# Layer-1 attention rebuilt: four heads in row and column groups of the array

## The reference, cut to what matters

```python
q = x @ Wq.T + bq; k = x @ Wk.T + bk; v = x @ Wv.T + bv
qm = q.reshape(d_batch * NB_HEADS, q_len, d_head)      # 16 heads of width 8, 256 tokens
att = jnp.einsum('nqd,nkd->nqk', qm, km)
att = jax.nn.softmax(att, axis=-1)
att_out = jnp.einsum('nqk,nkd->nqd', att + batch_pos, vm)   # a bias added after the softmax
att_out = att_out.reshape(d_batch, q_len, d) @ Wo.T + bo
att_block = layer_normalize(att_out + x)
ff = (att_block @ W1.T + b1) @ W2.T + b2
return layer_normalize(ff + att_block)
```

## Time and profile before

| what | us |
|---|---|
| median of 3 runs | 1746.96 |
| lowest, highest | 1745.7, 1750.88 |
| the profiled execution, its own time | 1739.43 |
| its span, first to last instruction | 1737.6 |
| first and last start of a score matmul (L1716) in it | 1224.0, 1610.3 |

### The profile page before, as it was taken

How to read it: one execution, slowest core, us unless ns; L and a number is a source line. 1 busy time by engine, 2 the same in 40 slices (tenths; PEclk the granted TensorE clock), 3 DMA queues, 4 the chain that set the end, 5 groups by cost and what they waited for, 6 DMA issues and landing times. The chain is left out here.

```text
span 1737.6 us, 31729 instructions
## 1 busy us (share of the span) xinstructions
PE 1351.8 (78%) x8970; PEld 1077.2 (62%) x8970; DVE 1112.3 (64%) x2581; ACT 939.1 (54%) x2747; POOL 812.6 (47%) x824
## 2 busy tenths in 40 slices
PE   2267786697877984897998998994899988999552
PEld 0044564464645764897998897992566666676452
DVE  4575787877978544648447547442578888888522
ACT  1155564565756763666666666662556555555110
POOL 2446646555475312564665564663344544432103
PEclk7588898888988986999999999996889899989576
DMA  6300000000000005020020000006111111220063
GB/s 211 106 2 3 1 9 3 7 9 0 8 2 7 9 7 205 20 109 10 10 103 15 11 12 8 13 9 193 35 22 31 26 24 34 33 31 10 12 194 112
DMA packets 127182, 72.28 MB, mean 42 GB/s; under 512 B 78296, under 2 KB 118488, under 8 KB 126680
## 3 DMA queue, kind: packets, MB, share of 16 engines
q1 hardware_dynamic: 116664, 60.95, 12.3%
q0 software_dynamic: 3200, 6.56, 1.5%
q10 hardware_dynamic: 7200, 3.41, 0.7%
HBM read 53.26 MB, written 17.12 MB: 41 GB/s over the span
## 5 line engine op out<-in xcount | busy, mean ns | idle before, releaser
L1433 POOL TENSOR_TENSOR hl<-hid,hh 128x256 fp32r<-128x256 f32 x396 | 293.2, 742 | 221.2 <-ACT hh L1410 217.4
L1476 DVE SCALAR_TENSOR_TENSOR hid<-GU,gub,sg 128x256 f32<-128x256 f32 x396 | 190.3, 481 | 194.5 <-ACT sg L1404 111.8
L1304 PE MATMUL GU<-xh,wh 128*128 128x256 f32 x792 | 233.5, 295 | 39.4 <-DVE wl L1452 30.3
L1404 ACT ACTIVATE sg<-GU,gub 128x256 f32<-128x256 f32 x396 | 188.2, 475 | 123.6 <-PE GU L1306 122.1
L1305 PE MATMUL GU<-xl,wh 128*128 128x256 f32 x792 | 225.6, 285 | 0.0
L1306 PE MATMUL GU<-xh,wl 128*128 128x256 f32 x792 | 225.6, 285 | 0.0
L1840 ACT ACTIVATE prob<-S,negmax 128x256 f32<-128x256 f32 x256 | 119.2, 470 | 164.3 <-DVE negmax L2225 162.2
L1304 PEld LDWEIGHTS GU<-xh,wh 128*128 128x128 f32 x792 | 152.4, 192 | 48.9 <-issue 27.1
L1410 ACT CAST hh<-hid 128x256 fp32r<-128x256 f32 x396 | 158.1, 399 | 27.0 <-DVE hid L1476 25.8
L1716 PE MATMUL S<-kpad,qn 128*128 128x512 f32 x256 | 152.0, 679 | 1.5 <-POOL kpad L1960 1.4
L1305 PEld LDWEIGHTS GU<-xl,wh 128*128 128x128 f32 x792 | 152.8, 193 | 0.0
(11 more groups left out here) (289 smaller groups left out, 3263.9 us busy)
## 6 DMA issues: line engine op xcount, KB each, us to landing
raw<-in_expert_w SPq DMA_DIRECT2D x4, 2688.0 KB, 12.3
modb<-mod_d SPq DMA_DIRECT2D x2, 2688.0 KB, 15.0
list<-zero SPq DMA_DIRECT2D x5, 1024.0 KB, 9.7
raw<-in_expert_w SPq DMA_DIRECT2D x4, 1152.0 KB, 6.6
wa<-in_w SPq DMA_DIRECT2D x16, 256.0 KB, 3.5
wb<-in_w SPq DMA_DIRECT2D x16, 256.0 KB, 4.3
kpad<-rel_d SPq DMA_DIRECT2D x1, 3072.0 KB, 13.3
qkv_d<-qkvT SPq DMA_DIRECT2D x24, 128.0 KB, 4.5
```

The costliest lines, as they stand in the source:

```text
L1304: pe.matmul(out, lhs[0], rhs[0], start=start, stop=False, skip_group_check=True)
L1404: act.activation(sg[:, c % BUFS], GU[c % BUFS][:, 0:TT], ACT.Silu, bias=gub[:, GATE, e * CH0 + c:e * CH0 + c + 1]).then_inc(silu, 1)
L1433: pool.tensor_tensor(hl[:, b], hid[:, b], hh[:, b].bitcast(F32), ALU.subtract).then_inc(hid_lo, 1)
L1476: dve.scalar_tensor_tensor(out=hid[:, c % BUFS], in0=GU[c % BUFS][:, TT:2 * TT], scalar=gub[:, UP, e * CH0 + c:e * CH0 + c + 1], in1=sg[:, ...
```

## The change

`RowBank`, the slots and their loop are gone. `Turns` orders the uses of a bank by a number, and every engine walks through 109 steps written out in full, 8 to a row; `row_at(step, offset)` says which row has a given piece of work in a step. A step carries half a quad: two of the 16 heads, for all 256 queries.

- Keys and queries lie as `KA` and `QA`, each head in its own group of 32 partitions: 8 rows of features and a ninth. Four heads (a quad) stand one above the other.
- `scores` issues eight matmuls in a step: four for the scores by query into `S` (two heads), which only serve the maximum, and four for the scores by key into `ST` (two heads of four steps earlier), which feed the exponential. The four heads lie in four different groups of rows.
- `maxima` takes one reduction over 1024 elements a partition. `tops` (on PE and DVE) transposes the negated maxima and adds them into the ninth row of `QA`, where the ninth row of `KA` is one, so that scores by key come out with the maximum already subtracted.
- ACT takes one exponential over 1024 elements a step. The transposes of the probabilities, their copy, the sums, the reciprocals and the pass of `add_bias` over the probabilities are gone.
- `av` uses V as weights, nine columns for each head (the ninth is one and yields the sum), and runs four heads in four groups of columns: eight matmuls with the bias `B` moving, eight with the probabilities moving. ACT copies the result to `OE`.
- SP sends `qkv` out in 6 DMAs and reads `KA`, `QA` and `vT` back in 9; it sends `OE` out in 8 and reads `ol` back in 2. Division by the sum and the sum of both parts happen afterwards on 128 x 256 (steps 1 to 3 of `step_a`).
- Q, K and V come from two matmuls with hT as weights and 384 columns moving, and DVE adds their bias (`add_bias`, now another function). The padded keys are gone from POOL; the mixing of layer 0's expert outputs moves from DVE to POOL (`mix_outputs`), and POOL now waits for `w_in` before it gathers.

```diff
+        bankE = Turns(sem("te_full"), sem("te_drained"), {"hT": -9.5, "qkv0": -8.5, "qkv1": -7.5, "vT": 3.5, "pos": 29.5})
+        bankL = Turns(sem("tl_full"), sem("tl_drained"), {"oT": 17.5, "wo": 18.5, "router": 27.5, "aT": 20.5, "uT": 21.5, "w2": 22.5})
+        bankN = Turns(sem("nm_full"), sem("nm_drained"), {"top0": 2, "top1": 4, "top2": 6, "top3": 8, "h2T": 26.5})
...
+            def step_program(step):
+                b = row_at(step, -7)
+                if b is not None:
+                    bankE.wait_emptied(sp, "qkv1", b)
+                    of = io["qkv_d"][b].rearrange("(k d) (l c) -> l k d c", d=ROWS, c=16)
+                    for t in range(TILES):
+                        for k in range(3):
...
                     take_waits(sp, taken)
-                    sp.dma_start(io["att_d"][bass.ds(l, 1)].rearrange("o (p x) -> (o p) x", p=P), attT[:]).then_inc(att_out, 16)
-                    sp.wait_ge(att_out, 16 * (l + 1))
+                    if b >= 2:
+                        sp.wait_ge(t_mm, STEPS * (b - 1))
                     take_waits(sp, taken)
-                    if not known_zero(l):
-                        bankL.wait_full(sp, "wo", slot - 1)
+                    for k, to in ((K_, KA), (Q_, QA)):
+                        for j in range(4):
+                            sp.dma_start(to[32 * j:32 * j + ROWS, b % 2],
+                                         io["qkv_d"][b, k * ROWS:(k + 1) * ROWS].rearrange("d (g j x) -> d g j x", j=4, x=NT)[:, :, j]).then_inc(qk_in, 16)
+                    bankE.wait_full(sp, "vT", b - 1)
                     take_waits(sp, taken)
...
-                if E:
-
-                    bankE.wait_emptied(sp, "v", slot)
+                    sp.dma_start(vT[:], io["qkv_d"][b, V_ * ROWS:V_ * ROWS + DH1].rearrange("d (h x) -> (d h) x", x=NT)).then_inc(v_in, 16)
+                b = row_at(step, 13)
...
+                    of = io["o_d"][b].rearrange("(o d) (g j x) -> d g j o x", d=ROWS, j=4, x=NT)
+                    for j in range(4):
+                        for o in range(2):
+                            sp.dma_start(of[:, :, j, o], OE[32 * j:32 * j + ROWS, b % 2, :, o * NT:(o + 1) * NT]).then_inc(o_sent, 16)
+                    sp.wait_ge(o_sent, 128 * (b + 1))
                     take_waits(sp, taken)
-                    if not known_zero(b):
-                        sp.wait_ge(reord, 2 * b)
-                        take_waits(sp, taken)
-                        sp.wait_ge(k_pad, 4 * b)
+                    if b >= 1:
+                        sp.wait_ge(dA, NA * (b - 1) + 3)
                     take_waits(sp, taken)
-                    sp.dma_start(qkvs[:], io["qkv_d"][bass.ds(b * 3, 3)].rearrange("k (p x) -> p k x", p=P)).then_inc(qkv_in, 16)
-                    sp.wait_ge(qkv_in, 16 * (b + 1))
-                    take_waits(sp, taken)
-
-            over_rows(sp, slot_program)
...
+            def scores(step):
+
+                s, t = halves_at(step)
+                if s:
+                    row, i = s
+                    if i == 0:
+                        pe.wait_ge(qk_in, 128 * (row + 1))
+                        if row == 0:
+                            pe.wait_ge(B_out, B_STEPS)
+                    if STEPS * row + i > 0:
+                        pe.wait_ge(s_max, STEPS * row + i)
+                if t:
+                    row, i = t
+                    if i % 2 == 0:
+                        bankN.wait_emptied(pe, f"top{i // 2}", row)
+                    if STEPS * row + i > 0:
+                        pe.wait_ge(t_exp, STEPS * row + i)
+                for blk in range(2):
+                    for e in range(2):
+                        if s:
+                            row, i = s
+                            j, g = 2 * (i % 2) + e, i // 2
+                            mm = pe.matmul(S[:, e, blk * NT:(blk + 1) * NT], QA[32 * j:32 * j + DH1, row % 2, g, blk * P:(blk + 1) * P],
+                                           KA[32 * j:32 * j + DH1, row % 2, g, :], start=True, stop=True)
+                            if blk == 1 and e == 1:
+                                mm.then_inc(s_mm, 1)
+                    for e in range(2):
+                        if t:
+                            row, i = t
+                            j, g = 2 * (1 - i % 2) + e, i // 2
+                            mm = pe.matmul(ST[:, e, blk * NT:(blk + 1) * NT], KA[32 * j:32 * j + ROWS, row % 2, g, blk * P:(blk + 1) * P],
+                                           QA[32 * j:32 * j + ROWS, row % 2, g, :], start=True, stop=True)
+                            if blk == 1 and e == 1:
+                                mm.then_inc(t_mm, 1)
+
+            def tops(row, quad):
+                pe.wait_ge(s_max, STEPS * row + 2 * quad + 2)
+                bankN.wait_drained(pe, f"top{quad}", row)
+                for q in range(2):
+                    mm = pe.transpose(NM[:, q * P:(q + 1) * P], top_now[:, quad % 2, q, :], ident)
+                mm.then_inc(bankN.full, 1)
+
+            def av(row, quad):
+                if quad == 0:
+                    bankE.wait_emptied(pe, "vT", row)
+                if QUADS * row + quad > 0:
+                    pe.wait_ge(o_out, QUADS * row + quad)
+                for kb in range(2):
+                    for j in range(4):
+                        head = 4 * quad + j
+                        pe.matmul(O[32 * j:32 * j + ROWS, NT:2 * NT], V[:, row % 2, kb, head, :],
+                                  B[:, head, P * (1 - kb):P * (1 - kb) + NT], start=(kb == 0), stop=(kb == 1), skip_group_check=True)
+                pe.wait_ge(t_exp, STEPS * row + 2 * quad + 2)
+                for kb in range(2):
+                    for j in range(4):
+                        mm = pe.matmul(O[32 * j:32 * j + ROWS, 0:NT], V[:, row % 2, kb, 4 * quad + j, :],
+                                       pT[:, quad % 2, j, kb, :], start=(kb == 0), stop=(kb == 1), skip_group_check=True)
                 mm.then_inc(o_mm, 1)
 
```

```diff
+                    row, i = t
+                    act.wait_ge(t_mm, STEPS * row + i + 1)
+                    done = QUADS * row + i // 2 - 1
+                    if i % 2 == 0 and done > 0:
+                        act.wait_ge(o_mm, done)
+                    first = 2 * (1 - i % 2)
+                    act.activation(pT[:, (i // 2) % 2, first:first + 2].rearrange("p j k q -> p (j k q)"),
+                                   ST[:].rearrange("p e x -> p (e x)"), ACT.Exp).then_inc(t_exp, 1)
+                now = quad_at(step, 6)
+                if now:
+                    row, quad = now
+                    act.wait_ge(o_mm, QUADS * row + quad + 1)
+                    if row >= 2 and quad == 0:
+                        act.wait_ge(o_sent, 128 * (row - 1))
+                    act.copy(OE[:, row % 2, quad, :], O[:]).then_inc(o_out, 1)
+                b = row_at(step, 28)
+                if b is not None:
+                    act.wait_ge(dB, NBS * b + 11)
+                    act.activation(ex[:], lm[:], ACT.Exp).then_inc(g_exp, 1)
+
...
+            def mix_outputs(b):
+                weights = keep["mixw"][:, b * TILES:(b + 1) * TILES, :, None].broadcast_to([P, TILES, 2, D])
+                pool.wait_ge(gathered, 64 * (b + 1))
+                pool.tensor_tensor(ya[:], ya[:], weights, ALU.mult).then_inc(mix, 1)
...
+            def maxima(row, i):
+
+                dve.wait_ge(s_mm, STEPS * row + i + 1)
+                quad = i // 2
+                if i % 2 == 0 and QUADS * row + quad >= 2:
+                    before = QUADS * row + quad - 2
+                    bankN.wait_full(dve, f"top{before % QUADS}", before // QUADS)
+                first = 2 * (i % 2)
+                to = top_now[:, quad % 2].rearrange("p q (j c) -> p j q c", j=4)[:, first:first + 2, :, DH1]
+                dve.tensor_reduce(to, S[:].rearrange("p e (q k) -> p e q k", q=2), X, ALU.max, negate=True).then_inc(s_max, 1)
+
+            def tops(row, quad):
+                bankN.wait_full(dve, f"top{quad}", row)
+                of = QA[:, row % 2, quad, :]
+                dve.tensor_tensor(of, of, NM[:, 0:NT], ALU.add).then_inc(bankN.drained, 1)
+
...
+            def add_bias(b, t):
+                bankE.wait_full(dve, f"qkv{t}", b)
+                if t == 0 and b >= 1:
+                    dve.wait_ge(qkv_out, 96 * b)
+                dve.tensor_tensor(qkv[:, t, :], TE[:, 0:3 * D], b3[:], ALU.add).then_inc(bankE.drained, 1)
+
...
+            at_e = {-14: (1, 2, 3), -11: (4, 5, 6), -9: (7,)}
+            at_a = {17: (1, 2, 3), 19: (4, 5, 6), 20: (7, 8), 23: (9, 10, 11), 24: (12, 13, 14)}
+            at_b = {25: (1, 2, 3), 26: (4, 5, 6), 28: (7, 8, 9, 10, 11), 29: (12, 13, 14, 15), 30: range(16, 29)}
...
+            def step_program(step):
+                s, _ = halves_at(step)
+                if s:
+                    maxima(*s)
+                now = quad_at(step, 2)
+                if now:
+                    tops(*now)
```

(61 more changed lines are left out.)

661 lines of the change are left out of this document (269 added, 392 removed).

## The result

The changed kernel takes 1723.83 us (median of 11 runs, 1716.86 to 1730.35), the kernel before 1745.7 (11 runs on the same chip, 1733.58 to 1750.88): ratio 0.987, 95% interval 0.984 to 0.989. It is faster by 22 us, 1.3 per cent, where 106 were forecast, and lies above the range. Its profiled execution took 1716.86 us, with a span of 1715.1; it is the fastest of the 11.

A forecast was written before the change was run, and what follows sets the result against it. DVE, with PE close behind, bounds the kernel; a full row falls from 51.5 to 38 us (30.3 DVE, 3.6 waits, +2 clock, +2 disturbances). Heads -116, start +6, end +4: 1633, forecast 1640; range 1595 to 1700.

The forecast's parts named there:

- a quarter: Share of time PE sits at the lower clock level in a full row, against a seventh before; +2 us a row.
- PE at the lower clock: Rival, chance 0.08: nearly the whole stretch at the lower level, scores 2.3, `av` 3.9, row 51 us plus waits; 1755.
- row groups run four at a time: Scores on PE: a step's 16 records in four groups of 32 rows take 1.2 us; bounds 1.1 and 4.5.
- DVE's reduction: Maxima on DVE: each reduction of 1024 elements takes 1.22 us, eight make 9.8 us a row.
- ACT's exponential: ACT in a row: 8 exponentials of 1.08 us, 14 us with copies and small ones; never last.
- SP's chain: SP's DMA issues and landings within a row: 22 us, with seven of eight steps, 33 us, to hide in.
- PE's small products: PE in a row: some 9 us of small products, from 44.6 less scores, `av` and transposes.
- four same-step waits: PE waits for DVE's result in steps 1 (`att`), 2, 5 and 0: 1.5, 0.5, 0.9, 0.7, together 3.6 us a row.
- The end: From the last `av` to Wo: 11 us instead of 7.1, with 8 issues, 2 issues and two landings; +4.
- The start: Before the first scores: POOL gathers behind `w_in`, mixing follows, 15 issues instead of 4; +6 us.
- two at a time: Rival, chance 0.12: only two row groups run together, scores take 2.3 us; row 44, 1685.
- Waits cost more: Rival, chance 0.16: same-step waits or SP's chain cost 10 us a row instead of 3.6; row 45, 1690.

The follow-up runs named there:

- k32: Changed kernel with the scores' matmuls over all 32 rows of each group, the added rows holding zeros; 1673.82 us, ratio to before 0.957.
- k16: Changed kernel with the scores over 16 rows of each group instead of 8 and 9, the added rows holding zeros; 1688.23 us, ratio to before 0.966.
- nobias: Changed kernel with the eight `av` matmuls on the bias `B` left out, so the result lacks the position bias; 1712.57 us, ratio to before 0.979.
- bias2: Changed kernel with the eight bias matmuls of `av` issued twice; 1711.55 us, ratio to before 0.979.
- lateonly: Changed kernel with only the three small PE groups (oT, h2T, positions) issued one step later, behind the next scores; 1685.33 us, ratio to before 0.965.
- late: Changed kernel with scores over 32 rows, POOL gathering before `w_in`, and three small PE groups behind the next step's scores; 1645.17 us, ratio to before 0.943.
- early: Changed kernel with POOL waiting for `w_in` only before its first mixing, no longer before its first gather; 1716.18 us, ratio to before 0.982.
- late2: As late, with the second Q, K, V matmul also moved behind the next step's scores; 1642.16 us, ratio to before 0.939.

## Why the prediction was wrong

**The step that failed is the clock of PE.** The prediction let PE sit at the lower level for "a quarter" of the time and gave that +2 a row. It is 0.70 of the stretch of the heads (granted clock 0.65). Scores at 2.1 us and `av` at 3.6 came as the rival *PE at the lower clock* had them (2.3 and 3.9), though not its 51 us a row: rows 3 to 5, the full ones, took 45.8, 44.2 and 40.7 us instead of 38. The rival had been put at 0.08 because today's heads showed 0.91. That argued from a kernel whose scores and `av` fill all 128 rows to one whose scores fill 8 and 9 of each 32. k32 gives 40 of the heads' 65 us back by filling rows with zeros, k16 lies between, and nobias and bias2 move the clock by the full-row matmuls beside the scores. The rate was right, the share was not. At 1.3 us a row for each tenth of the time, 0.70 in place of 0.25 makes some 6 us a row by this estimate, 38 + 6 = 44, and rows 3 to 5 took 43.6 in the mean. In k32 the share of time at the higher level over the heads went from 0.30 to 0.64 and the rows 0 to 6 became 4.2 us shorter in the mean, 1.2 a tenth.

The Trainium skill (TensorE: Matmul & The Clock Gate, Part 1) ties the lower clock to the engine's pauses. lateonly agrees: PE idle for 44.1 us of its heads instead of 53.8, and 0.71 instead of 0.65. k32 shows that pauses are not all: the count of matmuls is the same, PE is idle for 70.3 us, and the clock is 0.82.

**With the clock back, most of a row stands as forecast.** From one row's first reduction to the next, by the starts of L2019 and its like (us):

| row | 0 | 1 | 2 | 3 | 4 | 5 | 6 |
|---|---|---|---|---|---|---|---|
| forecast | 25 | 26 | 30 | 38 | 38 | 38 | 35 |
| changed kernel | 32.0 | 30.9 | 43.7 | 45.8 | 44.2 | 40.7 | 45.6 |
| k32 | 30.5 | 29.2 | 38.3 | 41.6 | 38.3 | 38.2 | 37.5 |
| late | 31.8 | 27.9 | 35.0 | 33.6 | 33.3 | 34.5 | 32.6 |

Rows 3 to 5 of k32 are 39.4 in the mean against 38. That this is so close is in part luck: DVE has 27.0 us of work in a row where 30.3 were counted (from start to start, so with gaps; in that sum the 7.1 for small steps should be 7.8, 37 instructions at 0.21), and the wait for `att` is 3.9 us where 1.5 were counted. Rows 0 to 2 took 17 us more together than forecast even so, and no run here shows why.

**Point by point.** That row groups run four at a time was right: 1.15 us for 16 records, against 1.2 taken and 4.5 as the upper bound. So were DVE's reduction (1226 ns against 1.22 us) and ACT's exponential (1023 ns against 1.08 us). SP's chain was hidden. For PE's small products the prediction took some 9 us from today's 44.6 less scores, `av` and transposes; that subtraction leaves nothing (18.3, 16.4 and 10.9 us, since records overlap), while the row's small groups add up to some 8 us, so the term stands by them. Of the four same-step waits, 3.6 a row, the one for `att` was under-sized. Moving three of them gave 23 us with 32 rows, where 2.9 a row had been counted; but only some 14 us of that are pauses, about what was counted, and the rest is the clock. The end was +4 and is +15.3. Of these, 10.0 lie before Wo: the eight issues alone take 6.5 us of the 11 that were counted for both sets of issues and both landings. Another 4.0 lie between Wo and POOL's last `rsB` (19.2 us against 15.2) and 1.3 behind that; the prediction had nothing for either, and why they are there stays open. The start was +6 and is +12.6, of which 1.7 came before the block began and 10.9 in it. early takes 8.7 of these back, so the wait of POOL for `w_in` was the larger part. The rival *two at a time* is out by the 10 ns between four records. *Waits cost more* was half right. The result lies 24 us above the range's upper end; k32, with nothing changed but zeros in the spare rows, lies inside the range, though above the forecast's own 1615 to 1670.

## What to carry to other kernels

Before a matmul is cut down to few rows, ask what that does to the granted clock, for all of PE's work in the stretch: read PEclk in windows, and compare a version with the same matmuls over padded rows, which cost nothing in their own time here (fastest record 373 ns with 8 rows, 374 with 32). If a change leaves the slack engines waiting for PE while PE is "busy", look at the durations of single records before believing that PE has work to do. In a program where every engine walks in a fixed order, put a small product whose operand is made in this step behind the next step's large ones, and look at what else stands there in the first round: late2 put one behind 11.75 us of one-time work.

## What the runs showed of the hardware that was not expected

- In this kernel the granted clock moved with the rows that the matmuls fill, zeros included. In the stretch 1237 to 1560 it was 0.65 with 8 and 9, 0.73 with 16, 0.81 with 32, 0.54 with 8 and 9 and half of the full-row `av` matmuls gone, 0.76 with these issued twice. Columns of weights in `av` (9 or 32, beside scores over 32 rows) made no difference, 0.81 and 0.82.
- More matmuls need not make a kernel slower: with 512 records more, PE's busy time in the stretch was 266 us against 271, and the median 12 us less, with intervals that touch.
- Four row groups run fully side by side: at the higher level four fp32 records of 256 columns start within some 20 ns, and the next four some 0.21 us later. A step's 16 records took 1.15 us, against 4.5 by today's price of records one after another, 3.9 times less. The Trainium skill (TensorE: Matmul & The Clock Gate, Part 3) has 3.07 times for four groups; the 12 us that the prediction derived from it do not show here.
- A DMA issue of 36 pieces of 1 KB (`o_d`) keeps SP's queue for 0.8 us, eight of them for 6.5.
